# A third layer's first image: both softmax halves ahead of its products, last output products in the banks of the scores, VectorE's work in another order

## The reference

```python
# the layer before (attention over pixels), its last step
h = einsum('oc,bct->bot', w_proj, h) + b_proj;  y = x2 + h
# the third layer: per image
h = groupnorm(x) * norm_w + norm_b                       # 32 groups
q, k, v = (h.T @ qkv_w.T + qkv_b)                        # (B, N, 8 heads, 32) each
attn = softmax(einsum('bnhd,bngd->bnhg', q, k) * 32**-0.5)   # 8 x 8 for each pixel
o = einsum('bnhg,bngd->bnhd', attn, v)
out = x + (o @ proj_w.T + proj_b).T
```

## Time and profile before

| | us |
|---|---|
| median of 3 runs | 1891.13 (1889.68 to 1892.18) |
| the profiled execution | 1891.69 |
| its span (first to last instruction) | 1889.9 |
| third layer, from its first scores (1484.01) to the end of the span | 405.9 |

### The profile page before, as it was taken

One profiled execution on the slowest core, in us unless ns is written; L12 is line 12 of the kernel. 1 busy time (PEld: TensorE's weight loads), 2 busy tenths in 40 slices (PEclk: granted clock), 3 DMA queues, 4 the chain that ended last, 5 costly groups with the idle time before them and its releaser, 6 DMA issues.

```text
span 1889.9 us, 37123 instructions
## 1 busy us (share of the span) xinstructions
PE 1655.2 (88%) x15160; PEld 766.2 (41%) x15160; DVE 1375.5 (73%) x2121; ACT 790.7 (42%) x1542; POOL 1360.5 (72%) x581
## 2 busy tenths in 40 slices
PE   5898656799999999999999999999999868989974
PEld 2333223344344344444444444344444535555541
DVE  5777577887877777877777777777775157878875
ACT  0443410255445445445545445455456523333320
POOL 0684500298787887887887887887887748989996
PEclk8898877799999999999999999999999999999996
DMA  5000030300001001001001001001001021222211
GB/s 192 1 2 1 1 131 0 128 36 24 2 2 68 1 2 68 2 2 68 2 1 69 1 2 69 2 2 68 2 1 69 27 93 48 78 74 76 75 51 48
DMA packets 48431, 75.10 MB, mean 40 GB/s; under 512 B 30804, under 2 KB 31110, under 8 KB 48262
## 3 DMA queue, kind: packets, MB, share of 16 engines
q1 hardware_dynamic: 38758, 72.15, 10.7%
q10 hardware_dynamic: 9504, 0.59, 0.3%
HBM read 44.87 MB, written 25.17 MB: 37 GB/s over the span
## 4 chain that ended last, share of the span: by engine, by line
PE 58%; DVE 31%; issue 5%; ACT 3%; POOL 2%; DMA 1%; POOLq 0%; SPq 0%; DVEq 0%; ACTq 0%
DVE MX L1361 19%; PE AV L697 8%; PE RB L776 6%; PE AV L785 3%; PE S L733 3%; PE S L645 3%; PE RB L733 3%; PE RB L1015 3%; DVE HI L1338 2%; DVE LO L1339 2%; PE RB L751 2%; PE RB L723 2%; PE S L994 1%; DVE BN L1395 1%; PE S L707 1%
## 5 line engine op out<-in xcount | busy, mean ns | idle before, releaser
L1271 POOL TENSOR_TENSOR ACC<-ACC,PR 128x1024 f32<-128x1024 f32 x360 | 843.5, 2383 | 24.9 <-ACT PR L1135 24.7
L1135 ACT ACTIVATE PR<-S 128x512 f32<-128x512 f32 x682 | 386.2, 604 | 382.1 <-PE S L683 297.8
L1361 DVE TENSOR_REDUCE MX<-S 128x1 f32<-128x512 f32 x661 | 431.5, 680 | 107.2 <-PE S L645 55.7
L1271 POOL TENSOR_TENSOR ACC<-PR 128x1024 f32<-128x1024 f32 x72 | 169.6, 2377 | 355.6 <-PE S L712 156.8
L697 PE MATMUL AV<-PR,VT 128*32 128x512 f32 x2304 | 304.8, 607 | 2.0 <-ACT PR L1135 2.0
L645 PE MATMUL S<-HI 32*128 32x512 f32 x661 | 259.3, 482 | 18.0 <-DVE MX L1361 11.8
L1135 ACT ACTIVATE PR<-RB 128x512 f32<-128x512 f32 x320 | 190.4, 604 | 102.6 <-PE S L683 42.1
L1361 DVE TENSOR_REDUCE MX<-RB 128x1 f32<-128x512 f32 x298 | 199.7, 679 | 26.0 <-PE RB L645 15.1
L668 PE MATMUL S<-HI 32*128 32x512 f32 x682 | 193.3, 465 | 2.4 <-DVE X L1554 2.3
L1297 POOL TENSOR_TENSOR PR<-WO,WRK 128x1792 f32<-128x1792 f32 x32 | 155.4, 4873 | 49.8 <-DVE ENC L1713 32.6
L645 PEld LDWEIGHTS S<-HI 32*128 32x128 f32 x661 | 105.8, 187 | 189.3 <-DVE MX L1361 82.8
(11 more groups left out here) (362 smaller groups left out, 3462.0 us busy)
## 6 DMA issues: line engine op xcount, KB each, us to landing
X<-out_y SPq DMA_DIRECT2D x24, 1024.0 KB, 5.0
out_y<-X SPq DMA_DIRECT2D x16, 1024.0 KB, 5.3
X<-in_x SPq DMA_DIRECT2D x8, 1024.0 KB, 8.4
OHU<-out_y SPq DMA_DIRECT2D x8, 512.0 KB, 4.2
X<-out_y SPq DMA_DIRECT2D x8, 512.0 KB, 4.0
out_y<-X SPq DMA_DIRECT2D x8, 512.0 KB, 3.1
out_y<-OHU SPq DMA_DIRECT2D x8, 512.0 KB, 3.1
WO<-WO SPq DMA_DIRECT2D x128, 16.0 KB, 1.8
```

What stands on the lines that cost most here:

```text
L1135: nc.scalar.activation(exps(s, pair)[:, HALF * one:HALF * one + HALF], RING[ring.place()], ACT.Exp, scale=1.0 if i is None else float(D) * ...
L1271: nc.gpsimd.tensor_tensor(ACC[:, pair, :], so_far, exps(s, pair), ALU.add).then_inc(pool_used, 1)
L1361: nc.vector.tensor_reduce(out=MX[:, h, t, keys:keys + 1], in_=bank(), op=ALU.max, axis=AX.X).then_inc(ring_free, 1)
```

## The change

It touches the third layer's first image only, apart from one semaphore that is split in two.

- PE: `scores3(0, 1)` moves from step 3 of image 0 to the place ahead of the last of the four `first_values`. The wait for `half_kept` after `sums` goes. The four output products move from step 4 to step 5, behind `transpose3(0)` and `group_sums(0)`, and use the four banks of S4, after a wait for `centre(0, 1)` (`s_used3`). `scores3(1, 0)` then waits until the residuals have read them.
- ACT: `apply3(B + 1)` one place forward, `exp3(0, 1)` ahead of `keep_sums`, `keep_p(0, 0)` ahead of `return_inverse` with a wait for `weigh(0, 1)`.
- DVE: `centre(0, 1)` and `weigh(0, 1)` directly behind those of half 0; `invert` behind `products(0)`; `statistics` stays and `normalise` goes behind it in step 4; residuals in steps 5 and 6, there behind the outputs and products of the step; the second `group_stats` behind them.
- SP: `share(0, 1)` ahead of the wait for `y_ready`; `p_in3` becomes one semaphore for each half.

```diff
@@ SP @@
                     share(0, 0)
                     next_xin(2)
+                    share(0, 1)
                     sp.wait_ge(y_ready, B)
                     load_xres(1)
                     load(out_d[B - 1], XRES, y_out)
-                    share(0, 1)
@@ PE @@
             for n in range(MT // 2):
+                if n == 3:
+                    scores3(0, 1)
                 first_values(n)
             ring.only(RING_LAST)
             sums(2 * (2 * B + 1) + 1)
-            pe.wait_ge(half_kept, 2 * (2 * (2 * B + 2)))
...
-                    if b == 0 and k == 4:
-                        for half in range(2):
-                            for o in range(CT):
-                                output_product(o, half, B - 1)
...
+                    if b == 0 and k == 5:
+                        ring.only(0, 1, 2, 3)
+                        wait(pe, s_used3, 2)
+                        for half in range(2):
+                            for o in range(CT):
+                                output_product(o, half, B - 1)
+                        posted = drained.now()
+                        ring.only(RING_LAST)
-                    if b < B and k == 3:
+                    if 0 < b < B and k == 3:
                         scores3(b, 1)
                     if b < B - 1:
                         if k == 7:
+                            wait(pe, ring_free, posted)
                             scores3(b + 1, 0)
@@ ACT @@
             keep_first(2, AV[:, :])
+            apply3(B + 1)
             keep_first(3, FRONT)
+            exp3(0, 1)
             keep_sums(2 * (2 * B + 1) + 1)
-            apply3(B + 1)
+            act.wait_ge(p_ready3, 2)
+            keep_p(0, 0)
             return_inverse(2 * (2 * B + 1) + 1)
-            keep_p(0, 0)
```

## The result

| | before | after |
|---|---|---|
| median | 1891.36 us (4 runs, 1889.68 to 1892.18) | 1880.60 us (4 runs, 1879.69 to 1881.66) |
| profiled execution, its span | 1891.69, 1889.9 | 1881.66, 1879.9 |
| second group sum on PE | 1547.84 | 1536.49 |
| tile 4 on GpSimd | 1550.04 | 1538.70 |

The ratio is 0.9944 (95% interval 0.9931 to 0.9957). The gain is 10.8 us; 15.1 was forecast. The time lies within the stated range (1870.5 to 1884.5), but just outside the forecast's own interval of 1871 to 1880, which had a chance of 0.70. At tile 4 the gain was 11.34 us; the end of the span came 10.0 us earlier.

The account below looks back on a forecast made before the run. GpSimd's tile 4, held by the second group sum, was taken as the bound. 15.9 us earlier there, less 0.8 for the sums' trip (0.5) and output products (0.3), gave 15.1 us: 1876.0 median, range 1870.5 to 1884.5.

Parts of the forecast that it names:

- Which wait ends last: GpSimd in the third layer: tile 4 waits for norm factors behind the second group sum, a wait of about 15 us.
- Step 1: PE's scores3(0,1) ahead of the last values costs 2.49 us; the DMA of the sums moves from 1496.19 to 1498.68.
- Step 2: DMA of the sums takes 1.94 us to the reciprocal, 0.5 allowed for the image load; ACT is free at 1501.5.
- Step 3: PE's q/k units from ACT's start: unit 1 at 1502.85, 3.34 us per q unit, units 5 and 6 at 1516.4 and 1519.4.
- rival A: Smaller gain of 10 to 12 us: PE's 1.7 us idle leaves units at the lower clock; 1880 to 1881, chance 0.12.
- Step 4: First group sum at 1521.55, four output products at 1.72 us each, second group sum at 1532.0 instead of 1547.84.
- Products 2 and 3 follow without a gap: GpSimd's products 2 and 3 start at 1507.6 and 1512.5, removing waits of 19.17 and 11.31 us.
- Time won before 1550 should stay won: After 1550 GpSimd is at work 92% of the layer, so the 15.1 us at tile 4 reaches the end.
- Rival E: No change: something other than GpSimd sets the pace of the images and the gain is given back; 1891, chance 0.05.
- GpSimd's waits behind tile 4: GpSimd's waits between tile 4 and the last stay at 24 us; differing by more than 4 would refute the prediction.
- Rival B: More than the sum: GpSimd's 6.8 us DMA wait, with PE's stall in the scores, does not recur; 5.4 us more, 1870.6, chance 0.05.
- Rivals C and D: C: GpSimd never stops, tile 4 at 1519, 1860, chance 0.03. D: PE stays at the lower clock, 1899.8, chance 0.05.

Follow-up runs that it names:

- gate: The changed kernel with ScalarE's return of the inverse behind the units of step 1 and the four output products behind the second group sum: 1874.7 us, ratio 0.9909.
- both_late: The changed kernel with the return of the inverse behind the second block's q/k units and the image load behind share(0,1): 1875.7 us, ratio 0.9913.
- half_load: The changed kernel with the image load cut in two, 512 KB ahead of the sums and 512 KB behind share(0,1): 1876.5 us, ratio 0.9927.
- both_exp: both_late with ScalarE's exp of image 1's first half ahead of the keep of image 2's first unit: 1879.5 us, ratio 0.9935.
- after_again: The changed kernel as it is, profiled once more: 1881.1 us, ratio 0.9952.

## Why the prediction was right, and where it was off

- *Which wait ends last* ("What matters is when tile 4 can start"): right for this change. The new gate was named, and its wait of "about 15 us" measured 15.01.
- *Step 1*: DMA of the sums at 1498.68, measured 1498.48. Right.
- *Step 2, "1.94 us until the reciprocal", with 0.5 allowed*: **the step that failed.** It was 4.98, 2.54 us over the allowance and 1.5 over the upper bound. The bound was also added up wrongly: a trip that waits until 1501.1 and then takes its 1.94 ends at 1503.0, which is 2.4 us late, not 1.5. And 1501.1 was too early even for the trace of before, where the load, issued at 1496.46, took 5.3 us to land. After the change the load was issued 0.9 us later too, at 1497.36, and landed 5.6 us after that, at 1502.96. The question that decides is which of the two is issued first, not how full the DMA engines are.
- The Trainium skill (DMA: Bandwidth & Descriptors, section on queues, rings and completion order) was read there for its turns packet by packet, which "would put the delay at a few tenths". Measured: 3.0 us. The same section says that the write that counts a transfer as done lands only behind every earlier write of its DMA engine, across its queues; the rows here (a trip that ends with the load, in each of the ten cases issued 0.05 us or more behind it) agree with that sentence, which the prediction didn't use. No run tells it from a turn that lasts as long as the load does.
- *Step 3, rival A's mechanism*: the pause grew from 1.7 to 5.01 us, and the next unit took 3.64 instead of 1.93. This 1.71 us was priced in rival A only. The units behind it ran in 1.93, as step 3 said.
- *Step 4*: output products 1.74 us apart (1.72 taken), second group sum 10.3 us behind the first (10.45 and 0.3 taken). Right. "Products 2 and 3 follow without a gap" was wrong for 3, at no cost.
- The sum, with the two costs put in and the 0.3 for the output products taken out again: 1532.8 + 2.54 + 1.71 - 0.3 = 1536.75, less 0.39 for the layer's earlier start: 1536.36; measured 1536.49. That is the whole miss at tile 4. The likeliest case of the prediction thus lost to what it called A, with the trip beyond A's bound, and the time (1880.6) is A's. Two of the prediction's own signs of being wrong came true: a trip over 3.5 us (4.98) and a q/k unit over 3 us after 1502 (3.64). That the time is within the range is owed to A, which the range was stretched to hold.
- *"Time won before 1550 should stay won"*: nearly, by two errors of opposite sign. From tile 4 to the end of the last product 3.3 us were lost, 3.1 of them by tile 7, at PE's lower clock; the last projection came at the higher clock (1.95 us instead of 3.75), which gave back 2.0. And gate shows the limit of the claim: another 6 us at tile 4 bring nothing at tile 7. Rival E ("something else than GpSimd sets the pace") was false for the first 17 us of gain at tile 4 (64.4 before, 47.0 in both_late) and true for the next 6.
- GpSimd's waits behind tile 4: 27.2 us against 24, within the 4 named. But they changed their releaser: 20.3 us for the DMA of the weights and 3.6 for VectorE before, 0.6 and 26.6 now.
- Rival B: its stall did recur. PE still waited 2.36 us inside the scores (2.32 before), and GpSimd 7.16 us (6.79 before).
- Rivals C and D: excluded by the wait of 15.01 us, and by units of 1.93 us from 1510.77 on.

The end of the trace, the last two projections of PE before and after:

```profile
1876.18 3.78 PE L1015 MATMUL RB<-ACC,X 128*128 128x512 f32 x4 [0.47 <-ACT ACC L1197]
1880.89 3.75 PE L1015 MATMUL RB<-ACC,X 128*128 128x512 f32 x4 [0.94 <-DVE OHU L1722]
```

```profile
1868.16 3.57 PE L1015 MATMUL RB<-ACC,X 128*128 128x512 f32 x4 [0.47 <-ACT ACC L1205]
1872.66 1.95 PE L1015 MATMUL RB<-ACC,X 128*128 128x512 f32 x4 [0.94 <-DVE OHU L1732]
```

## To carry to other kernels

When a step with a small DMA on its chain is moved, look for the next large transfer on the other queue too and compare the issue times: here, 0.27 us ahead of the load the small one took its 1.94 us, and 0.06 us behind it 5.24, the load's whole time. Don't let an engine that others wait for stand in the queue behind such a trip; moving the return out of the way won 7.0 us more (1873.6 against 1880.6). And a gate stays the gate only up to the next one: price the gain against the second-latest chain too.

## What the runs showed of the hardware

- An 8 KB transfer that takes 1.93 to 2.07 us alone took 3.60 to 5.37 us when it was issued 0.05 to 1.79 us behind a load of 1 MB on the other queue, and ended 0.1 to 1.1 us behind its landing; at 0.02 us behind (once) and ahead of it, no delay. Behind a load of 512 KB at 1.80 us it took 1.98.
- A pause of PE of 2.0 us (half_load) was followed by a unit of 3.51 us and one of 5.01 (after) by 3.64 instead of 1.93; one of 3.22 us (both_exp) by two spread matmuls of 2.04 instead of 1.12. But not every such pause was: behind one of 2.73 us the unit took 3.64 in after and 1.93 in both_exp.
- Of one and the same kernel, the granted clock in the 12 us from 56 us behind the first centre on was 0.50 in one execution (after) and 0.71, 0.72 and 0.86 in its three thirds in another (after_again); the layers were 3.5 us apart.
